# Moving three pieces of side work in a fused attention and expert kernel: copies of x, products of the projected matrix, the first pair's sums

## The reference, cut to what matters

```python
xn = layernorm(x)
# attention without softmax, 32 heads of 16
qkv = relu(einsum('bnc,oc->bno', xn, qkv_weight))      # q, k, v
vk = einsum('bnhe,bnhd->bhed', concat([v, 1]), k)      # sum over all tokens of a sequence
vk_q = einsum('bhed,bnhd->bnhe', vk, q)
y1 = (vk_q[..., :16] / (vk_q[..., 16:] + eps)) @ proj_weight.T + proj_bias
# experts
spikes = sigmoid(xn @ enc_w + enc_b)                   # 512 -> 1024
cont = spikes @ s2c_w + s2c_b                          # 1024 -> 64
comb = top-2 of softmax(router(cont))                  # 8 experts
moe = sum over the two experts of their two layers on cont
dec = sigmoid(sigmoid(moe @ c2s_w + c2s_b) @ dec_w + dec_b)
out = x + y1 + layernorm(dec) * ln_g + ln_b
```

## Time and profile before

| | |
|---|---|
| median of 3 runs | 1892.42 us (1892.19 to 1892.52) |
| the profiled execution's own time | 1892.0 us |
| its span, first to last instruction | 1890.3 us |
| mean granted TensorE clock | 0.994 of full speed |
| TensorE busy | 98% of the span |
| VectorE busy | 66% |
| ScalarE busy | 43% |
| GpSimd busy | 22% |

### The profile page before, as it was taken

How to read it: one execution, slowest core, us unless ns; L and a number is a source line. 1 busy time by engine, 2 the same in 40 slices (tenths; PEclk the granted TensorE clock), 3 DMA queues, 4 the chain that set the end, 5 groups by cost and what they waited for, 6 DMA issues and landing times. The chain is left out here.

```text
span 1890.3 us, 25374 instructions
## 1 busy us (share of the span) xinstructions
PE 1846.1 (98%) x8792; PEld 1527.1 (81%) x8792; DVE 1243.2 (66%) x2344; ACT 815.3 (43%) x1407; POOL 408.5 (22%) x467
## 2 busy tenths in 40 slices
PE   7999999999999998999999999999999999999997
PEld 6888888888788887887788788888888888888886
DVE  6555565564565887883898755666666666666667
ACT  4555545555222443432787623333333333333333
POOL 2000000000003554540100142222222223333331
PEclk9999999999999999999999999999999999999999
DMA  6642424533313443432788522222222222222211
GB/s 226 241 192 111 195 95 179 203 140 131 121 57 142 151 150 136 151 137 68 208 249 276 158 85 72 95 94 95 94 94 95 94 95 79 81 92 84 95 51 67
DMA packets 105149, 244.70 MB, mean 129 GB/s; under 512 B 30576, under 2 KB 52928, under 8 KB 97472
## 3 DMA queue, kind: packets, MB, share of 16 engines
q1 hardware_dynamic: 96752, 234.53, 34.7%
q0 software_dynamic: 8272, 8.57, 1.6%
HBM read 160.47 MB, written 82.58 MB: 129 GB/s over the span
## 5 line engine op out<-in xcount | busy, mean ns | idle before, releaser
L639 DVE TENSOR_TENSOR spl<-sp_t,sph 128x512 fp32r<-128x512 f32 x128 | 88.6, 692 | 189.4 <-ACT sph L445 189.4
L111 PE MATMUL AB_E<-xs,enc_h 128*128 128x512 f32 x512 | 208.1, 406 | 3.4 <-DVE xs L627 3.4
L113 PE MATMUL AB_E<-xs,enc_h 128*128 128x512 f32 x512 | 200.6, 392 | 0.0
L112 PE MATMUL AB_E<-xs,enc_l 128*128 128x512 f32 x512 | 200.3, 391 | 0.0
L1898 PE MATMUL D_D<-dec_h,rateh 128*128 128x512 f32 x512 | 200.1, 391 | 0.0
L1899 PE MATMUL D_D<-dec_l,rateh 128*128 128x512 f32 x512 | 199.8, 390 | 0.0
L1900 PE MATMUL D_D<-dec_h,ratel 128*128 128x512 f32 x512 | 199.3, 389 | 0.0
L441 ACT ACTIVATE sp_t<-AB_E,cols 128x512 f32<-128x512 f32 x128 | 88.2, 689 | 208.1 <-PE AB_E L113 205.3
L1030 POOL DMA_INDIRECT slots_scratch<-ctok,idx x128 | 129.6, 1013 | 216.0 <-DVE part L1347 98.7
L1741 POOL DMA_INDIRECT ga<-eo_scratch,idx x64 | 66.4, 1037 | 485.3 <-DVE ratel L2004 466.2
L1797 ACT ACTIVATE rate<-D_Y,cols 128x512 f32<-128x512 f32 x128 | 87.9, 687 | 120.8 <-PE D_Y L1879 120.8
(11 more groups left out here) (421 smaller groups left out, 4756.4 us busy)
## 6 DMA issues: line engine op xcount, KB each, us to landing
xs_scratch<-xs SPq DMA_DIRECT2D x16, 2048.0 KB, 8.1
xsd<-xs_scratch SPq DMA_DIRECT2D x15, 2048.0 KB, 7.9
xs<-xs_scratch SPq DMA_DIRECT2D x14, 2048.0 KB
wt<-ew_scratch SPq DMA_DIRECT2D x39, 513.0 KB, 3.8
xd<-in_x SPq DMA_DIRECT2D x16, 1024.0 KB, 5.4
out_y<-out SPq DMA_DIRECT2D x64, 256.0 KB, 2.0
x<-in_x SPq DMA_DIRECT2D x15, 1024.0 KB, 5.4
xf_scratch<-xt SPq DMA_DIRECT2D x11, 1024.0 KB, 10.1
```

The source lines that it names most:

```text
L111: pe.matmul(out, w_hi, x_hi, start=start, stop=False)
L112: pe.matmul(out, w_lo, x_hi, start=False, stop=False)
L113: return pe.matmul(out, w_hi, x_lo, start=False, stop=stop)
L639: dve.tensor_tensor(T["spl"][:, n % 3, :], T["sp_t"][:, m % 2, :], f32(T["sph"][:, n % 3, :]), ALU.subtract)\
```

## The change

Three moves, with the amount of arithmetic unchanged.

1. ScalarE's full copy `xt` of a turned chunk leaves `turn` for a function of its own, `keep`, called one encoder tile later (the copy of the last chunk in tile 0 of the next block). It waits for VectorE's low half (`xl_out`); VectorE no longer waits for the copy; TensorE waits for it (`xt_out`) before it writes to the bank again, two turns later.
2. The four products of the projected matrix lie at tiles 36, 38, 40 and 42, one for each pair, where they were at 36, 37, 38 and 39, two for each; the key sums are spread at tile 44 where it was 40.
3. The sums of the first pair follow tile 14's value on VectorE where they followed tile 15's, their `high` follows tile 14 on ScalarE, and their `low` lies between tile 15's key and value on VectorE.

```diff
@@ front, scalar
                 act.activation(xs[i % 2][:, 0, c, :], bT[c % 2][:, :], ACT.Copy).then_inc(S["xh_out"], 1)
+
+            def keep(i, c):
+
                 if i in IN_PAIRS:
                     k = IN_PAIRS.index(i)
+                    act.wait_ge(S["xl_out"], i * KC + c + 1)
                     if c == 0:
                         wait(act, S["xt_stored"], 16 * (k - 1))
                     act.activation(T[f"xt{k % 2}"][:, c, :], bT[c % 2][:, :], ACT.Copy).then_inc(S["xt_out"], 1)
...
                 for m in range(HC):
                     encode(i, m)
+                    if m == 0 and i:
+                        keep(i, KC - 1)
+                    if i + 1 < NB:
+                        if i == 0 and m > 4:
+                            keep(1, m - 5)
+                        elif i and m in (2, 4, 6):
+                            keep(i + 1, m // 2 - 1)
@@ front, tensor, turn
                 wait(pe, S["xl_out"], n - 1)
+                wait(pe, S["xt_out"], sum(k // KC in IN_PAIRS for k in range(n - 1)))
@@ front, vector, turn
                 dve.wait_ge(S["xh_out"], i * KC + c + 1)
-                if i in IN_PAIRS:
-                    dve.wait_ge(S["xt_out"], IN_PAIRS.index(i) * KC + c + 1)
@@ keyvalue
-        X_RANK, X_CNT, X_TURN, X_M, X_KS = RANK_AT, RANK_AT + 1, CLOSE_AT + 2, CLOSE_AT + 4, CLOSE_AT + 8
+        X_RANK, X_CNT, X_TURN, X_KS = RANK_AT, RANK_AT + 1, CLOSE_AT + 2, CLOSE_AT + 12
+        X_M = range(CLOSE_AT + 4, X_KS, 2)
@@ keyvalue, beside of scalar, tensor and vector alike
-                if X_M <= n < X_M + KC:
-                    project_act(act, T, S, 1, 0, n - X_M, bX)
+                if n in X_M:
+                    project_act(act, T, S, 1, 0, X_M.index(n), bX)
@@ keyvalue, scalar
             for n in range(PAIR0):
                 single(n)
-            for s in range(4):
-                high(Q0, s)
+                if n == PAIR0 - 2:
+                    for s in range(4):
+                        high(Q0, s)
@@ keyvalue, vector
+                if n == PAIR0 - 1:
+                    for s in range(4):
+                        low(Q0, s)
                 value(n, bank(n, 1)[:, :], n)
                 weight_sums(n)
-            sums(Q0)
-            for s in range(4):
-                low(Q0, s)
+                if n == PAIR0 - 2:
+                    sums(Q0)
```

More of the change, by code:

```diff
@@ L1214, in beside @@
                     turn_pe(pe, T, S, 0, bX)
-                if X_M <= n < X_M + KC:
-                    wait(pe, S["ml_out"], n - X_M)
-                    project_pe(pe, T, S, 0, n - X_M, bX)
+                if n in X_M:
+                    wait(pe, S["ml_out"], X_M.index(n))
+                    project_pe(pe, T, S, 0, X_M.index(n), bX)
                 if n == X_KS:
@@ L1323, in beside @@
                         .then_inc(S["wl_out"], 1)
-                if X_M <= n < X_M + KC:
-                    project_dve(dve, T, S, 1, 0, n - X_M, bX)
+                if n in X_M:
+                    project_dve(dve, T, S, 1, 0, X_M.index(n), bX)
             def sums(q):
```

## The result

The change makes the kernel faster: median 1877.27 us (1876.16 to 1878.58, 4 runs) against 1892.47 us (1892.19 to 1894.59, 4 runs) of the kernel before beside it, a ratio of 0.9917 with an interval of 0.9903 to 0.993. The forecast was 1876.3 us. The profiled execution took 1876.74 us and its span is 1875.0, 15.3 us less than before; the forecast span was 1874.2.

A forecast was written before the change was run, and what follows sets the result against it. TensorE, busy for 98% of the span, was taken to bound the kernel. Savings of 5.0 + 8.6 + 2.5 = 16.1 us gave 1876.3 us; the forecast's own range was 1874 to 1878, with 1873.9 to 1881.5 as outer ends.

The forecast's parts named there:

- Part 1: Encoder block boundaries: full copies of x one tile later save 0.45 us for each of 11 blocks, 5.0 us.
- Rival 4: Encoder: moving the copies does nothing, because another chain ends at the same time; 1881.3 us, chance 0.05.
- The waits: Encoder: ScalarE's new wait before each copy and TensorE's third wait before 58 turns, both costed at 0.
- rivals 5 and 6: ScalarE's new wait: 5, 0.28 to 0.45 us a copy, no measurable change, chance 0.04; 6, longer wait, 1898 us, chance 0.03.
- rival 3: Encoder: TensorE's third wait shows at every turn, 3.5 us lost, 1879.8 us; chance 0.08.
- Part 2: Pairs 18 and 19: one product a pair removes stalls of 4.37 and 4.27 us, together 8.6 us.
- Rival 1: Four product pairs: VectorE falls behind as each `ml` waits for ScalarE; 3.1 us given back, 1879.4 us, chance 0.11.
- Part 3: First pair: sums beside tiles 14 and 15 remove TensorE's wait for the first `ss`, 2.5 us.
- Rival 2: Tile 15: early roundings make a late key or value and TensorE waits there; 2.5 us lost, 1878.8 us, chance 0.08.
- A clock that falls in a new place: Sign of a wrong prediction, anywhere in the kernel: the clock falls in a place where it did not before; no size given.

The follow-up runs named there:

- same_tile: Changed kernel with ScalarE's full copy back in the tile of its turn, still behind VectorE's low half; median 1877.74 us, before beside it 1892.96.
- three_subs: Changed kernel with VectorE's subtraction for each of the four products made three times; median 1880.82 us, before beside it 1892.96.
- only_sums: Kernel before with only the third move, the first pair's sums beside tiles 14 and 15; median 1889.54 us, before beside it 1892.60.
- low_last: Changed kernel with the first pair's low halves behind tile 15's value again, sums and roundings still early; median 1878.77 us, before beside it 1892.96.
- changed_again: The changed kernel run once more, unedited, in the session of its separate parts; median 1879.13 us, before beside it 1892.60.
- only_copies: Kernel before with only the first move, the full copies of x one tile later; median 1888.49 us, before beside it 1892.60.
- only_products: Kernel before with only the second move, one product a pair of tiles; median 1886.00 us, before beside it 1892.60.
- ml_first: Kernel before with the first product's rounding and subtraction ahead of the last key and value in both stalled pairs; median 1888.92 us, before beside it 1892.55.

## Why the prediction was right

- **Part 1, 5.0 us forecast, 4.56 measured.** The mechanism was right; the count was off by one. 0.45 us were saved at 10 boundaries, not 11: the one from block 0 to block 1 keeps its stall (same_tile). I took each move to be "one tile later" and did not look at what stands there in block 0. Rival 4, no gain at all, falls.
- **The waits, forecast 0.** ScalarE's new wait costs nothing, even where it is 0.87 us long (rivals 5 and 6 fall). The third wait on TensorE costs nothing, nor do four more (rival 3 falls), and that not only behind the long matmul that I read: half of the turns stand 0.11 us behind a short one, and their step did not change either. The Trainium skill ("Advanced Engine Details and Errata", section Network/Comms) gives 50 to 100 ns for a sequencer's reading of a semaphore. No run here shows such a cost in the open; whether the sequencer had read these semaphores ahead of the engine, or a reading costs less, these traces don't tell.
- **Part 2, 8.6 us forecast, 8.74 measured.** Rival 1 did not come in: four windows of 12.16. But the room was mis-sized: I had VectorE at 11.3 of 12.17 us with its wait for ScalarE, 0.9 to spare. Busy time and that wait are 10.56 + 0.58, and yet only 0.44 are to spare (three_subs): the 0.47 of idle time in front of `ss` belongs to VectorE's chain with ScalarE too. The split of one stall into 2.48 of idle time and 1.9 of clock and restart holds for that execution; where the clock stays full the same stall costs 2.77 (only_sums), 1.6 less. So the size of this term is in part luck: it was read from an execution in which the clock had fallen in both pairs.
- **Part 3, 2.5 us forecast, 2.45 measured** (with the restart 2.57). Rival 2 did not come in: the last of the four low halves ends 0.9 us before the first is read, where I had 0.5 (592.2 and 592.7). By low_last their early place is 0.7 of it.
- **Not in the sum: +0.61 us where the experts begin.** The first 10.4 us of that stage ran at a lower granted clock than before, 0.69 against 0.84, and 0.46 of the 0.61 are lost there: the clock had fallen by the start of that stretch, where before it fell 1.8 us into it. A clock that falls in a new place was among the signs of being wrong; this one fell earlier in a place where it fell already. Whether the change brings it is open. The stage lasts 188.4 to 189.0 us in eight of the nine traces whose kernel holds part 2, and 187.8 to 188.1 in the four without it, but low_last holds it and shows 187.84. The windows, first of the changed kernel, then of the kernel before:

```profile
873.73:884.14 10.41, 8.96 (x36) 7.06 (x37) 5.82 (x9) 4.42 (x9) 2.27 (x3) 0.69 0.88 278
```

```profile
889.59:900.00 10.41, 8.93 (x38) 6.99 (x39) 6.14 (x10) 4.77 (x9) 1.74 (x3) 0.84 0.87 278
```

16.1 less 0.44 in part 1, and 0.61 here, with 0.14 more in part 2 and 0.07 in part 3, is 15.26, the difference of the two executions. That the median too came within 1 us of the forecast is in part luck: the sum has no term for a clock that falls in other places, and the same kernel's median was 1879.13 in the session of changed_again, above the range of 1874 to 1878 that the forecast itself had.

**Open.** What decides whether the clock falls behind a given idle time. Behind the same wait for `ss`, 2.3 us each time, it stayed full in before and only_copies (first pair 7.90 and 7.86) and fell in only_products and ml_first (9.49 and 9.37). Behind the 1.5 and 1.6 us of ml_first's two pairs it stayed full; in the six stalled pairs of before, only_copies and only_sums, 2.4 to 2.5 us each, it fell five times. No run here tells what decides it.

## What to carry to other kernels

Where two engines read the same bank, let the one that the bound engine waits for go first, and hang the other's work behind it: here the wait was harmless on the engine that had slack, in either of the two tiles tried. Price a side job on a nearly full engine by its work and by the wait that comes with it, and take the wait away by giving the job to the engine one round later. A stall of TensorE costs its idle time for certain and the clock behind it only sometimes, so reckon both and keep the second in the range.

## What the runs showed of the hardware that I had not expected

The runs of the changed kernel spread from 1876.2 to 1879.5 us although three of its stages (encoder, first pair, pairs) repeat within 0.1 us, and one place shows how. At the start of the single tiles TensorE waits twice in both profiles, for its own sequencer 0.83 us (1.4 us behind the end of an earlier wait of 1.53) and then for VectorE's `v`. In the changed kernel's first profile the clock fell behind the first wait (start to start 0.43 us until 490.8); the second wait then is short, and the matmuls behind it run at the full rate, 0.24 us apart (first rows). In changed_again the clock stayed full behind the first wait, the second was longer for it, and the clock fell there (second rows, 0.43 apart):

```profile
492.64 0.36 PE L1208 MATMUL B_A<-v,kh 128*128 128x258 f32 x1 [0.88 <-DVE v L1299]
...
493.67 0.40 PE L284 MATMUL AB_E<-wv_h,xs 128*128 128x512 f32 x1
493.91 0.40 PE L285 MATMUL AB_E<-wv_l,xs 128*128 128x512 f32 x1
```

```profile
493.68 0.36 PE L1208 MATMUL B_A<-v,kh 128*128 128x258 f32 x1 [2.46 <-DVE v L1299]
...
495.29 0.63 PE L284 MATMUL AB_E<-wv_h,xs 128*128 128x512 f32 x1
495.72 0.63 PE L285 MATMUL AB_E<-wv_l,xs 128*128 128x512 f32 x1
```

A slow stretch ahead of a wait is swallowed by the wait; the same stretch behind it is paid: 102.55 against 100.95 us, 1.6 us, in "singles". (The two profiled executions differ by 2.55 us; another 1.05 lies ahead of the encoder's first row, 43.69 against 44.74.) Of all thirteen traces seven look like the first rows here and six like the second; no run tells what decides it. Second, VectorE's instructions of 0.68 us that follow each other start 0.60 us apart (729.44, 730.05 and 730.64 in three_subs), so a chain of these added up from their durations comes out an eighth too long.
